# The first two experts' up weights split in 16 pieces during the projection stage

## What is computed

```python
xn = layernorm(x)
Q, K, V = (spike(layer_norm(xn @ W.T + b, g, beta) - 1.0) for W in (Wq, Wk, Wv))
out = (Dh - hamming(Q, K) + log_pe_bias) * scale @ V         # 16 heads of 16, 4096 x 4096
s = spike(layer_norm(spike(out - 0.5) @ Wo.T + bo, go, betao) - 1.0)
r = rms_norm(xn, ffn_scale)
ids = argmin(dist2(r, centroids))                            # one of 8 experts a token
h = r @ up_w[ids]; a, g = split(h)                           # 256 -> 2 x 512
y = (a * silu(g)) @ down_w[ids]                              # 512 -> 256
result = x + s * silu(y + xn)
```

## Time and profile before

| | before |
|---|---|
| median of 3 runs | 391.56 us (388.51 to 393.59) |
| the profiled execution | 388.83 us |
| its span, first to last instruction | 387.0 us |
| granted TensorE clock, mean | 0.992 of full speed |
| PE busy over the span | 364.7 us (94%) |
| DVE busy | 315.9 us (82%) |
| ACT busy | 224.6 us (58%) |
| POOL busy | 234.7 us (61%) |

### The profile page before, as it was taken

The page is one execution under the profiler, slowest core; times in us unless marked ns, Lnnn a source line. Parts: engine busy times, 40 slices in busy tenths (PEclk is TensorE's granted clock), DMA queues, the critical chain, the costliest instruction groups (busy, mean ns, idle before and its releaser), DMA issues.

```text
span 387.0 us, 9389 instructions
## 1 busy us (share of the span) xinstructions
PE 364.7 (94%) x2583; PEld 307.6 (79%) x2584; DVE 315.9 (82%) x785; ACT 224.6 (58%) x611; POOL 234.7 (61%) x296
## 2 busy tenths in 40 slices
PE   8999999999969999985999999999999999999981
PEld 4878888888848888864888888888888888888871
DVE  5989999997688999997578777887877777777873
ACT  5589789888733333444455555555555555555551
POOL 4688777778601444786466666666666666666642
PEclk9999999999999999999899999999999999999998
DMA  6687768463398021539122222223222233321000
GB/s 212 199 303 204 220 180 285 145 180 98 104 207 222 29 83 41 153 96 307 34 72 87 67 67 71 80 86 95 76 81 82 79 95 89 92 78 55 29 16 0
DMA packets 31874, 45.44 MB, mean 117 GB/s; under 512 B 4113, under 2 KB 25810, under 8 KB 31716
## 3 DMA queue, kind: packets, MB, share of 16 engines
q1 hardware_dynamic: 25200, 29.73, 26.2%
q0 software_dynamic: 6416, 15.26, 13.6%
q10 hardware_dynamic: 228, 0.10, 0.1%
HBM read 36.84 MB, written 15.63 MB: 136 GB/s over the span
## 4 chain that ended last, share of the span: by engine, by line
PE 69%; DVE 9%; DMA 8%; issue 7%; ACT 3%; POOL 2%; ACTq 1%; SPq 1%; DVEq 0%; POOLq 0%
PE bank L632 20%; PE bank L450 16%; PE bank L650 10%; PE bank L511 4%; DMA row_a<-rows_a,slot_id 4%; PE bank L615 3%; PE bank L604 2%; DMA down_sb<-in_down_w 2%; PE bank L554 2%; PE bank L429 2%; PE bank L515 2%; ACT d_hi L825 2%; DVE d_lo L1218 1%; PE bank L523 1%; DVE up_lo L1172 1%
## 5 line engine op out<-in xcount | busy, mean ns | idle before, releaser
L1218 DVE TENSOR_TENSOR d_lo<-down_sb,d_hi 128x1024 fp32r<-128x1024 f32 x39 | 47.8, 1226 | 31.7 <-ACT d_hi L825 30.8
L1366 POOL DMA_INDIRECT row_a<-rows_a,slot_id x39 | 41.3, 1060 | 46.8 <-DVE e_o L1232 30.5
L825 ACT ACTIVATE d_hi<-down_sb 128x1024 fp32r x39 | 41.3, 1060 | 41.7 <-issue 26.3
L1399 POOL DMA_INDIRECT out_x<-e_o,slot_id x39 | 44.3, 1137 | 21.0 <-issue 14.5
L632 PE MATMUL bank<-up_hi,e_xh 128*128 x156 | 52.5, 418 | 0.0
L1372 POOL DMA_INDIRECT row_s<-rows_s,slot_id x39 | 39.7, 1018 | 15.6 <-issue 11.6
L632 PE MATMUL bank<-up_lo,e_xh 128*128 x156 | 48.9, 395 | 0.0
L632 PE MATMUL bank<-up_hi,e_xl 128*128 x156 | 48.6, 392 | 0.0
L807 ACT ACTIVATE e_xh<-bank 128x256 fp32r<-128x256 f32 x39 | 15.0, 384 | 40.9 <-PE bank L604 15.2
L753 ACT ACTIVATE junk<-bank 128x256 bf16<-128x256 f32 x96 | 35.4, 378 | 5.1 <-PE bank L450 4.7
L450 PE MATMUL bank<-w_hi,x_hi 128*128 128x264 f32 (+1 forms) x128 | 35.5, 359 | 0.0
(11 more groups left out here) (221 smaller groups left out, 979.2 us busy)
## 6 DMA issues: line engine op xcount, KB each, us to landing
up_raw<-in_up_w SPq DMA_DIRECT2D x16, 512.0 KB, 4.0
rows_a<-xn SPq DMA_DIRECT2D x32, 129.0 KB, 2.4
rows_a<-in_x SPq DMA_DIRECT2D x8, 512.0 KB, 11.6
down_sb<-in_down_w SPq DMA_DIRECT2D x8, 512.0 KB
xs<-in_x SPq DMA_DIRECT2D x7, 512.0 KB, 4.0
rows_s<-s_out SPq DMA_DIRECT2D x8, 256.0 KB, 2.5
blk_tab<-in_blocks SPq DMA_DIRECT2D x1, 1024.0 KB, 5.7
row_a<-rows_a,slot_id POOLq DMA_INDIRECT x39
```

The source lines that it names most:

```text
L825: act.activation(d_hi[:, :, :], down_sb[:, bass.ds(e, 1), :, :].rearrange("p a c n -> p (a c) n"), ACT.Copy).then_inc(d_high, 1)
L1218: V.tensor_tensor(d_lo[:, :, :], down_sb[:, bass.ds(e, 1), :, :].rearrange("p a c n -> p (a c) n"), d_hi[:, :, :].bitcast(F32), ALU.subtra ...
L1366: G.indirect_dma_start(row_a[s % 4][:, :], None, rows_a, bass.IndirectOffsetOnAxis(ap=slot_id[:, s:s + 1], axis=0), bounds_check=N - 1, oo ...
L1399: G.indirect_dma_start(out, bass.IndirectOffsetOnAxis(ap=slot_id[:, s:s + 1], axis=0), e_o[s % 4][:, :], None, bounds_check=N - 1, oob_is_ ...
```

## The change

ACT makes the high part of experts 0 and 1 in the projection stage, in 16 pieces of 128x256 (an expert, a half, a quarter), one at the end of each of the steps 9 to 24. DVE makes the low part of the same piece one step later, in steps 10 to 25, after the statistics and ahead of the three spikes. The ten instructions of the output bias go from the steps 9 to 18 to the steps 20 to 29. In the attention stage ACT and DVE make six experts in place of eight: ACT 2 and 3 after its last tile, then 4, 6 and 5 after the chunks 0, 1 and 3, and 7 as before; DVE 2 and 3 at chunk 4, 4 and 5 at chunk 5, 6 at chunk 6, none at chunk 7, and 7 as before. The loads of `up_raw` stay where they are; those of the first two experts count on semaphores of their own.

```diff
+EARLY = 2
+PIECE = D
+EARLY_FROM = 9
+EARLY_AT = {EARLY_FROM + n: (n // 8, n // 4 % 2, n % 4) for n in range(8 * EARLY)}
+HIGH_ORDER = (2, 3, 4, 6, 5, 7)
...
+            def early_high_part(e, half, q):
+                cols = slice(q * PIECE, (q + 1) * PIECE)
+                if half == 0 and q == 0:
+                    act.wait_ge(up_early[e], 16 * DC)
+                act.activation(up_hi[:, e, half, cols], up_raw[:, e, half, cols], ACT.Copy,
+                               scale=vc[:, FS_ + half:FS_ + half + 1]).then_inc(early_high, 1)
             for k in range(2, NT + 1):
                 step_a(k, 0)
+                if k in EARLY_AT:
+                    early_high_part(*EARLY_AT[k])
...
-            act.wait_ge(up_loaded, 16 * DC * E)
-            high_parts(0)
+            act.wait_ge(up_loaded, 16 * DC * (E - EARLY))
+            high_parts(2)
             keep_output_bias()
-            high_parts(1)
+            high_parts(3)
...
-                if c < NCH - 3:
-                    high_parts(c + 2)
+                if c in (0, 1, 3):
+                    high_parts({0: 4, 1: 6, 3: 5}[c])
...
+            def early_low_part(at, e, half, q):
+                cols = slice(q * PIECE, (q + 1) * PIECE)
+                dve.wait_ge(early_high, at - EARLY_FROM + 1)
+                last = V.scalar_tensor_tensor(up_lo[:, e, half, cols], up_raw[:, e, half, cols],
+                                              vc[:, FS_ + half:FS_ + half + 1],
+                                              up_hi[:, e, half, cols].bitcast(F32), ALU.mult, ALU.subtract)
+                if half == DC - 1 and q == 3:
+                    last.then_inc(up_ready, 1)
...
-                if 0 <= k - 9 < 10:
-                    output_bias(k - 9)
+                if 0 <= k - 20 < 10:
+                    output_bias(k - 20)
+                if k - 1 in EARLY_AT:
+                    early_low_part(k - 1, *EARLY_AT[k - 1])
...
-                    dve.wait_ge(up_high, DC * e + half + 1)
+                    dve.wait_ge(up_high, DC * HIGH_ORDER.index(e) + half + 1)
...
-                for e in {4: (0, 1), 5: (2, 3), 6: (4, 5), 7: (6,)}.get(c, ()):
+                for e in {4: (2, 3), 5: (4, 5), 6: (6,)}.get(c, ()):
```

More of the change, by code:

```diff
@@ L279, in build @@
         up_high, up_ready, ext_high = sem("up_high"), sem("up_ready"), sem("ext_high")
+        up_early, early_high = [sem(f"up_early{e}") for e in range(EARLY)], sem("early_high")
         hid_high, d_high, d_low = sem("hid_high"), sem("d_high"), sem("d_low")
@@ L335, in _ @@
                     e, half = UP_AT[t] // DC, UP_AT[t] % DC
-                    sp.dma_start(up_raw[:, e, half, :], up_w[e][half * P:(half + 1) * P, :]).then_inc(up_loaded, 16)
+                    sp.dma_start(up_raw[:, e, half, :], up_w[e][half * P:(half + 1) * P, :]) \
+                        .then_inc(up_early[e] if e < EARLY else up_loaded, 16)
             for g in range(NT // 4):
```

## The result

The changed kernel is slower by a little: ratio 1.0082 to the kernel before, with a 95% interval of 1.0053 to 1.0110 (20 runs of each, medians 393.58 and 390.6 us). On 390.6 us the ratio makes +3.2 us (+2.1 to +4.3); the medians themselves differ by 3.0. The forecast was +5.5 us. The median of before is 390.6 here and not the 391.56 of the three runs shown earlier. The ratio is what is used from here on; it leaves out one slow execution of the changed kernel, 397.42 us.

The account below looks back on a forecast made before the run. PE and DVE were taken as both full in the projection stage, the transfer as the hand-over's chain. 6.3 - 0.9 - 0.7 + 1.9 + 0.3 = +6.9, less 1.4, gave +5.5 us: 397.1 us, range 392.5 to 402.5.

Parts of the forecast that it names:

- DVE is full and pays each piece: Projection stage, steps 10 to 25: sixteen low parts at 0.39 us a slot add +6.3 us (4.8 to 7.7).
- The output bias: Projection stage: moving its instructions to steps 20 to 29 frees DVE, net -0.7 us (-1.2 to 0).
- POOL and DVE together: Projection stage: low parts wait behind POOL's sq, 0.12 us a piece on average, +1.9 us (0 to 8).
- the rival in which every piece waits half a microsecond: Projection stage: each piece meets POOL's sq or pow and waits 0.5 us or more; net +12.3, 403.9 us, chance 0.15.
- The slack of the stage: Projection stage: DVE's 0.6 us over four groups and PE's 0.4 us lead absorb -0.9 us (-0.5 to -1.5).
- ACT: Projection stage: high parts at 0.43 us a slot make ACT nearly full, not the bound; +0.3 us (0 to 1.5).
- The hand-over: Attention to experts: the last down-weight loads go at about 168.8 instead of 170.25; gain -1.4 us (-0.5 to -3.5).
- but the chain there is the transfer, and the first slot can't start before it lands: Hand-over, chunk 7: another 2.4 us of DVE work is gone, but it gains nothing because the transfer sets the start.
- PE's idle time keeps its length: Hand-over: PE's idle time before the first slot's hidden part stays about 4 us, since work ahead also moves up.

Follow-up runs that it names:

- e1: The change's sixteen pieces made into scratch buffers, attention stage still splitting all eight experts; ratio 1.0149 to the kernel before, stage 88.69 us.
- e8: The kernel before with only the output bias moved from steps 9 to 18 to steps 20 to 29; ratio 0.9990, stage 82.45 us.
- e7: Against the change, one expert early instead of two, low parts in steps 26 to 33, output bias not moved; ratio 0.9949 to the kernel before.
- e3: Against the change, only ACT's high parts in the projection stage, all low parts at full width in attention; ratio 1.0053 to the kernel before.
- e2: Against the change, no pieces in the projection stage, low parts of experts 0 and 1 left out; ratio 0.9945 to the kernel before.
- e4: The change with eight pieces of 512 columns, in every second step, instead of sixteen of 256; ratio 1.0117 to the kernel before.
- e6: The kernel before with only ACT's wait for the down weights moved to the first instruction that reads them; ratio 0.9990.
- e5: The change with ACT's wait for the down weights moved to the first instruction that reads them; ratio 1.0068 to the kernel before.
- e9: The change with POOL's gathers for slots 2 and 3 put behind the last chunk's norms; ratio 1.0079 to the kernel before.
- e10: The change with gathers behind the last norms and ACT's wait for the down weights moved later; ratio 1.0051 to the kernel before.

## Why the prediction was off in size

The direction and both places were right; the sum was +5.5 and the time rose by 3.2. The stage was to grow by 6.9 us and grew by 5.92 (e1: 5.97), and the hand-over was to give 1.4 and gave 2.3. By the terms of the sum:

- *DVE is full and pays each piece.* Right. Its sixteen steps were to last about 50 us and lasted 49.70. A slot was 0.37 us where 0.39 was taken: 5.9 us instead of 6.3 (16 x 0.39 is 6.2; the prediction rounded it up).
- *The output bias.* -0.7 was taken. Alone (e8) the move changes the stage by -0.1 to -0.3 us. In the change it frees more of DVE: the nine instructions in steps 10 to 18 took 1.5 us of its time before, two of them behind POOL's sq, and the six in steps 20 to 25 take 0.4, so -1.1. In the timeline of DVE, one of the two before, and then one of the six after:

```profile
58.52 0.60 DVE L984 TENSOR_TENSOR small<-small,b 128x8 f32<-128x8 f32 x1
```

```profile
83.28 0.16 DVE L989 TENSOR_TENSOR small<-small 128x4 f32<-128x4 f32 x1
```

- *POOL and DVE together.* +1.9 was taken. The piece was held up once by 0.4 us and lasted 489 ns on average against 450 untouched, some 0.6 us in all; another 1.3 us (5 x 0.256) fell on L920, which the prediction hadn't thought of. The size agrees by luck, since the place doesn't, and the rival in which every piece waits half a microsecond is out. The piece at 48.29 ended 0.28 us behind sq (49.14 and 48.86), less than its own 0.45, and so did the five in e7; so they were held up, but that they began only behind sq isn't shown. The lock rule of the Trainium skill (SBUF — State Buffer, "Who interferes with whom") would have it wait for all of sq.
- *The slack of the stage.* DVE's waits and PE's lead were put at 0.9 us. With 5.9 for the slots, 1.9 for the meetings with POOL and -1.1 for the bias, 6.7 us of work were added, and the stage grew by 5.92, so about 0.8 us found room: nearly as taken. Most of it isn't in the sixteen steps, in which DVE's steps grew by 6.16 us. The stretch from the last of the marks to the end of the stage (95.42 to 111.53, before 88.01 to 104.60) is 0.48 us shorter. The stage came out a microsecond below the sum by three small terms, the slot, the bias and ACT, and not by one.
- *ACT.* It was taken as nearly full and not the bound, with 0.3 us on top. e3 shows that alone it would cost 1.5 us of stage; here DVE never waits for it, so the 0.3 is nought. The slot was 0.40, taken as 0.43.
- *The hand-over.* This is the step that failed, and the larger miss for its size: -1.4 was taken, and 2.3 us came (e2: 2.33, the change: 2.29). "... but the chain there is the transfer, and the first slot can't start before it lands" had two things wrong. First, the transfer was taken to last as long as before. The loads do go 1.37 us earlier, as worked out, but from the first issue to ACT's gate it took 10.58 us instead of 11.50; at its old length the gain would have been the 1.4 of the prediction. Why it was shorter was not tested, and it took up to 11.61 us in kernels with the same order of loads (e4), so that part of the gain may be this execution's. Second, the transfer wasn't the only end. DVE's last s_out had ended 0.27 us ahead of ACT's gate before, and they moved by 1.93 us: e6 against e5 shows 1.92 of gain with the transfer out of the way. The s_out moved by POOL's norms. In the timeline of POOL, before and then after:

```profile
171.50 2.19 POOL L1358 TENSOR_TENSOR pv<-ss,eps 128x2 f32<-128x2 f32 x1
...
174.93 0.70 POOL L1360 TENSOR_TENSOR rs<-pv,half_neg 128x2 f32<-128x2 f32 x1 [0.18 <-POOL pv L1358]
```

```profile
178.41 0.19 POOL L1387 TENSOR_TENSOR pv<-ss,eps 128x2 f32<-128x2 f32 x1 [1.09 <-ACT junk L792]
...
179.99 0.70 POOL L1389 TENSOR_TENSOR rs<-pv,half_neg 128x2 f32<-128x2 f32 x1 [0.18 <-POOL pv L1387]
```

  The norms one chunk ahead of the last (L1358, L1387 after) had a pv of 2.19 us beside DVE's two splits before, and end at 175.63, 6.78 us behind at_done of chunk 7. With those splits gone the pv takes 0.19, and they end at 180.69, 4.63 us behind. The two gathers, the last norms and the last s_out follow on POOL and DVE, and end 11.39 us behind at_done instead of 13.32. But the splits of chunk 7 are the smaller part of it. e7 keeps them and has, like the change, one expert less at chunk 6. In its timeline of DVE and POOL:

```profile
172.89 2.47 DVE L1201 SCALAR_TENSOR_TENSOR up_lo<-up_raw,vc,up_hi 128x1024 fp32r<-128x1024 f32 x2
...
174.38 1.03 POOL L1387 TENSOR_TENSOR pv<-ss,eps 128x2 f32<-128x2 f32 x1 [1.08 <-ACT junk L792]
```

  The pv ends with the splits again (175.41 and 175.36; before, 173.69 and 173.64), but they start 0.87 us behind at_done and not 2.32, since DVE was done with the s_out of chunk 5 earlier. The last s_out end after 11.88 us. So of the 1.93 us by which s_out moved, 1.4 belong to the expert taken from chunk 6, which the prediction counted for the earlier loads only, and 0.5 to the one taken from chunk 7, which it put at nothing. Its "PE's idle time keeps its length" was wrong by 1.0 us, 3.09 against 4.11.

5.9 + 0.3 (PE's slower start of the attention stage, below) - 2.3 = 3.9 us by the stretches of the two profiled executions, which themselves differ by 4.0; two more differences nearly cancel, a first spike 1.01 us later and an expert stage 0.92 us shorter (202.71 us against 203.63, from PE's first instruction on a hidden part to the end of the span), and neither is shown to be the change's. The ratio says 3.2 with 1.1 on either side. What stays open is how much of the transfer's length comes from what shares its time.

## What to carry to other kernels

Work that is moved out of a stage is worth what the end of that stage gives back, and costs what the other stage's fullest engine can't take in beside its own work, step by step: here 2.3 us against 5.9, with one and the same instruction. Look for steps inside a loop that are lighter than the rest (here the last eight, without statistics) before spreading work evenly over all; half the move, put there, kept most of the gain at no cost. And where a chain runs through one transfer, look how near the second thing ends: removing the first alone can give next to nothing (e5, e6), and what moves the second may lie a chunk further ahead (e7).

## What was not expected of the hardware

PE's clock fell after an idle time that had left it alone in another execution. PE waits 2.22 us for DVE ahead of the attention stage's first matmuls, in the kernel before, and the matmuls of 512 columns that follow took 0.38 us; after the change it waits 2.23 us there, and they took 0.59 to 0.63 up to 121.8 us. It isn't the change that does it: e9 and e10 have the same projection stage and the same 2.22 and 2.23 us of waiting, and there the clock stayed at 1.00 and the stretch between the two marks at 64.25 and 64.24 us, as before (64.25; with the change 64.53). The busy time by stretches (columns as in the earlier trace rows), first of before, then of the changed kernel, then of e7:

```profile
112.20:114.00 1.80, 1.59 (x12) 0.62 (x12) 1.59 (x7) 0.00 (x0) 0.00 (x0) 1.00 1.07 238
183.40:185.90 2.50, 2.50 (x8) 2.17 (x9) 1.60 (x3) 0.89 (x2) 0.59 (x1) 0.50 0.26 76
```

```profile
119.20:121.80 2.60, 2.60 (x13) 0.89 (x14) 2.21 (x7) 0.00 (x0) 0.00 (x0) 0.50 1.08 203
188.30:190.80 2.50, 2.50 (x13) 2.15 (x14) 2.00 (x3) 1.37 (x3) 0.07 (x1) 1.00 0.37 108
```

```profile
113.80:119.00 5.20, 5.20 (x38) 3.49 (x36) 4.46 (x12) 0.00 (x0) 0.00 (x0) 0.50 1.13 213
```

The number behind the last bracket is the granted clock: 1.00 at the start of the attention stage before and 0.50, the lower of its two levels, in the change and in e7; the second line of the first two fences is the hand-over. In e7 it lasted over 5 us and put the whole attention stage 1.7 us back (65.97 us between the stretches against 64.25), which the time of e7 includes. At the hand-over it was the other way: 0.50 after 4.11 us of idle time before the change (and after 3.08 in e5), 1.00 after 3.09 us with it. So the length of an idle time alone doesn't tell which level follows. The length of the expert stage went with it: 202.4 us in e10, where the clock stayed at 1.00 behind the hand-over, and 205.7 in e5, where it was 0.50 for over 4 us. That is more than most of the differences measured here.
